# A two-layer vision tower with token routing: expert loads that wait for arithmetic instead of for written results, and a middle stage that begins three blocks later

## What is computed

```python
h = tok(x)                               # 64 patches of 28x28x3 through one matrix, class token, positions
h = h + attn0(layernorm(h))              # masked attention inside an image
h = h + ffn0(layernorm(h))               # 32 experts, 128 hidden, relu, the 2 best per token (sigmoid gates)
h = h + attn1(layernorm(h))              # |norm of (running sum - previous)| times a decaying sum of earlier tokens
h = h + ffn1(layernorm(h))               # 16 experts, 512 hidden, gelu, the 2 best per token (softmax gates)
```

## Time and profile before

| | us |
|---|---|
| three timed executions | 1088.7, 1091.51, 1091.65 (median 1091.51) |
| the profiled execution, its own time | 1087.39 |
| its span from first to last instruction | 1085.7 |
| busy in the span: PE / PEld / DVE / ACT / POOL | 914.5 / 772.5 / 847.8 / 503.9 / 678.9 |
| mean granted TensorE clock, as a share of 2.4 GHz | 0.909 |

### The profile page before, as it was taken

The page is one execution under the profiler, slowest core; times in us unless marked ns, Lnnn a source line. Parts: engine busy times, 40 slices in busy tenths (PEclk is TensorE's granted clock), DMA queues, the critical chain, the costliest instruction groups (busy, mean ns, idle before and its releaser), DMA issues.

```text
span 1085.7 us, 21714 instructions
## 1 busy us (share of the span) xinstructions
PE 914.5 (84%) x6064; PEld 772.5 (71%) x6064; DVE 847.8 (78%) x3318; ACT 503.9 (46%) x1342; POOL 678.9 (63%) x622
## 2 busy tenths in 40 slices
PE   6999999999999987476776877778569999999992
PEld 2577666677777666475665766677469989999992
DVE  1488889898888998666677899888667877778983
ACT  1355555555555442211112554777435655556561
POOL 1016666666676645677677767777777775545553
PEclk9999999999999997578887988877769999999996
DMA  9956566655566304577779973865188688889986
GB/s 371 353 206 217 202 217 222 222 201 201 201 206 211 123 21 116 152 209 206 210 219 310 293 259 120 265 228 169 59 302 263 231 253 277 275 279 301 356 325 235
DMA packets 118664, 246.57 MB, mean 227 GB/s; under 512 B 20914, under 2 KB 85936, under 8 KB 112400
## 3 DMA queue, kind: packets, MB, share of 16 engines
q1 hardware_dynamic: 77440, 191.26, 52.7%
q0 software_dynamic: 18592, 34.68, 9.4%
q10 hardware_dynamic: 22512, 19.25, 5.8%
HBM read 201.68 MB, written 45.43 MB: 228 GB/s over the span
## 4 chain that ended last, share of the span: by engine, by line
PE 39%; DVE 20%; issue 11%; DMA 11%; ACT 7%; SPq 6%; POOL 4%; ACTq 1%; DVEq 0%; POOLq 0%
PE ps L1032 6%; DMA xin<-lists_L 4%; PE ps L1010 4%; PE ps L762 4%; DMA results_L<-xin 3%; PE ps L1130 3%; POOL results_L L2582 3%; PE ps L829 3%; PE ps L1133 3%; PE ps L813 2%; SPq L614 2%; SPq L616 2%; PE ps L786 2%; SPq L607 2%; ACT x_hi L1211 2%
## 5 line engine op out<-in xcount | busy, mean ns | idle before, releaser
L2554 POOL DMA_INDIRECT lists_L<-rows,slots x230 | 263.4, 1145 | 153.3 <-issue 151.7
L2582 POOL DMA_INDIRECT results_L<-xin x145 | 146.2, 1008 | 96.3 <-DVE xin L2184 64.0
L2582 POOL DMA_INDIRECT results_L<-xin,place x146 | 144.1, 987 | 58.8 <-issue 39.3
L762 PE MATMUL ps<-xin,w_emb 128*128 128x512 f32 x292 | 137.7, 608 | 9.9 <-DMA w_emb<-in_w_main 8.3
L1032 PE MATMUL ps<-xin,QK 128*128 128x128 f32 x838 | 115.5, 289 | 2.6 <-DVE xin L2184 2.5
L1032 PEld LDWEIGHTS ps<-xin,QK 128*128 128x128 f32 x838 | 107.8, 204 | 4.5 <-issue 4.1
L2563 POOL TENSOR_TENSOR x_lo<-xin,x_hi 128x2048 fp32r<-128x2048 f32 x13 | 60.1, 4623 | 63.5 <-ACT x_hi L1219 63.1
L987 PE MATMUL ps<-ident,xin 128*128 128x128 f32 x291 | 66.3, 309 | 38.2 <-DMA xin<-lists_L 35.1
L1408 ACT ACTIVATE QK<-ps,xin 128x256 f32<-128x256 f32 x164 | 64.3, 475 | 70.9 <-PE ps L1010 70.9
L762 PEld LDWEIGHTS ps<-xin,w_emb 128*128 128x128 f32 x292 | 52.8, 194 | 58.9 <-issue 48.1
L2158 DVE TENSOR_SCALAR xin<-xin 128x128 f32<-128x128 f32 x291 | 92.7, 367 | 0.6
(11 more groups left out here) (408 smaller groups left out, 2436.4 us busy)
## 6 DMA issues: line engine op xcount, KB each, us to landing
xin<-in_x_main SPq DMA_DIRECT2D x48, 1536.0 KB, 6.7
xin<-in_w_L SPq DMA_DIRECT2D x81, 578.0 KB
xin<-in_w_L SPq DMA_DIRECT2D x98, 128.0 KB
xin<-lists_L SPq DMA_DIRECT2D x64, 132.0 KB
xin<-in_w_L ACTq DMA_DIRECT2D x65, 128.0 KB
x_hi<-results_L SPq DMA_DIRECT2D x13, 640.0 KB, 6.3
xin<-in_difference SPq DMA_DIRECT2D x13, 640.0 KB
xin<-in_distance SPq DMA_DIRECT2D x13, 640.0 KB, 6.6
```

What stands on the lines that cost most here:

```text
L762: mm = pe.matmul(psE[h], w_emb[:, k, :], xin[h][c][:, n, :], start=(k == 0), stop=False, skip_group_check=True)
L2554: pool.indirect_dma_start(out=lists[l.name], out_offset=bass.IndirectOffsetOnAxis(ap=slots_of(l, g, h)[:, t, k:k + 1], axis=0), in_=buf[:, ...
L2582: pool.indirect_dma_start(out=results[l.name], out_offset=bass.IndirectOffsetOnAxis(ap=where, axis=0), in_=yblk[u][:, q, :], in_offset=Non ...
```

## The change

Five edits, three of them in the way L1 blocks are fed:

1. `EARLY` is three blocks later: 48, 51, 57, 63, 69 instead of 45, 48, 54, 60, 66; `ALONE` goes with it.
2. DVE copies the places of L1 blocks too (81 more copies), and POOL's L1 results take their places from `place`.
3. The load of L1 block i waits for `y_ready` of block i-8, as that of L0 does, instead of `y_out`.
4. The fetches of finished results within the L1 blocks now wait for the landing of the results they read, which the waits of the loads before them had covered.
5. POOL does six instead of four scatters of group 11 before the first L1 result, and 14 instead of 16 between the results.

```diff
-        EARLY = {-3: 45, -2: 48, -1: 54, 0: 60, 1: 66}
+        EARLY = {-3: 48, -2: 51, -1: 57, 0: 63, 1: 69}
...
-            if l is L1:
-                eng.wait_ge(k.y_out[u], k.y0[u] + 16 * l.packets(i))
-            elif i >= l.unroll:
-                eng.wait_ge(k.y_ready, i - l.unroll + 1)
+            if i >= l.unroll:
+                eng.wait_ge(k.y_ready, k.i0 + i - l.unroll + 1)
...
-            sp_blocks(sp, L1, ends(load_end, 0))
-
-            def load_left(g, u, j):
+            def end_landed(g, u, j):
                 landed(L1, L1.enough(L1.class_of(g)))
                 load_end(g, u, j)
-            ends_left(load_left)
+            sp_blocks(sp, L1, ends(end_landed, 0))
+            ends_left(end_landed)
...
-                    if l is L0:
-                        dve.tensor_copy(place[:, u, :], xblk[u][:, :, PLACE].bitcast(U32))
+                    dve.tensor_copy(place[:, u, :], xblk[u][:, :, PLACE].bitcast(U32))
...
-                        where = place[:, u, q:q + 1] if l is L0 else xblk[u][:, q, PLACE:PLACE + 1].bitcast(U32)
-                            out=results[l.name], out_offset=bass.IndirectOffsetOnAxis(ap=where, axis=0),
+                            out=results[l.name], out_offset=bass.IndirectOffsetOnAxis(ap=place[:, u, q:q + 1], axis=0),
...
-                of = list(itertools.product((MG - 2, MG - 1), range(TILES * TOP)))[4:]
+                of = list(itertools.product((MG - 2, MG - 1), range(TILES * TOP)))[6:]
...
-            send(L1, MG - 2, MG % 2, 0, 4)
+            send(L1, MG - 2, MG % 2, 0, 6)
```

## The result

| | before | after |
|---|---|---|
| timed executions, median of five each | 1091.51 | 1083.02 |
| lowest and highest | 1088.14, 1091.93 | 1080.57, 1084.28 |
| profiled execution, its own time | 1087.39 | 1084.28 |
| its span | 1085.7 | 1082.5 |
| TensorE's mean granted clock | 0.909 | 0.903 |

The ratio is 0.9935, 95% interval 0.9915 to 0.9954: 0.65% or 7.1 us faster (the medians differ by 8.5, which lies within the interval). The forecast was 1084.5. The profiled executions differ by 3.1 us only: that of before lies 4.1 us under its median, that of after 1.3 above. So the two traces show where time moved, but not by themselves how large it is on average; the experiments give that.

The account below looks back on a forecast made before the run. Limits differ by stage: DVE, then POOL, then PE in L1, where late loads starve it and set the end. Terms -6.5 + 0 + 0 + 0 - 0.5 = -7.0 took 1091.51 to 1084.5 us; range 1080.0 to 1091.0.

Parts of the forecast that it names:

- Edits 2 and 3: L1 blocks: loads waiting for arithmetic, not landed results, remove PE's 11 waits for rows; -6.5 us, between 0 and -7.0.
- The copies: 81 place copies on DVE, 13.3 us of work, hidden before its waits for PE: 0, at most 1.6 us.
- up to 2.5 us later: L1 results on POOL: landing delay if the skill page's DVE lock held for these copies; loads would no longer wait for them.
- Edit 5: Start of L1 on POOL: two more scatters, 2.56 us, fit its 2.49 us idle before the first result: 0; uncovered 2.6.
- the one wait before load 24: L1: load 24's wait for scatters, left alone by the loads' edit; scatters would end up to 2.6 us sooner.
- Edit 4: SP in L1: waits for landings before fetches cost 0; at worst part of the 7.0 returns at few blocks.
- Edit 1: Middle stage three blocks later: start 5.2 us later, 4.7 given back, shorter stall -1.0; net -0.5, bounds -4.1 to +7.7.
- the shorter stall: DVE's 4.06 us idle before the first gather shortens because SP gets more head start: -1.0 us.
- B: Middle stage: the three blocks are only half given back, so the shift costs +2.9; net -3.6, 1087.9 us; chance 0.18.
- C: L1 loads: bound by transfers, so earlier loads only take longer; gain -1 to -3.5, near 1089 us; chance 0.12.
- D: Middle stage: group 1's slots come too late, POOL idles from about 668; net +1.2 to +4.4, 1092.7 to 1095.9; chance 0.08.
- E: L1: SP held by new landing waits or its fetches, loads start as late as before; 1091.51 within 1 or 2; chance 0.07.

Follow-up runs that it names:

- shift_only: The kernel before with only EARLY and ALONE three blocks later (48): 1091.53 us against 1089.46 for before timed together, ratio 1.0027.
- late_loads: The change with its L1 loads waiting for landed results again, all else as in the change: 1092.03 us, ratio to before 1.0029.

## Why the prediction was right, point by point

The time, 1084.5 forecast and 1083.02 measured, and the direction were right. Its terms were not as good as their sum.

**Edits 2 and 3, -6.5: the mechanism held, its size was off by 4.7.** Load 22 was to start at about 858.5, right behind the arithmetic; it starts 0.22 us behind it. PE's waits for rows were to fall under 1 us; none is left. But the gain is 11.1 to 11.2 us. The step that failed was "every one of the 11 waits should go, 7.0 us in all. At the most it is those 7.0": I took PE's row of waits as the upper end. It counts the times in which PE's records show a gap, 7.0 us in 11 times. PE's weight loads wait for the same DMAs in another row, which I had not used:

```profile
PEld ps L987 <- DMA xin<-lists_L: 10.8, 17, 2.1
```

That is 10.8 us in 17 times, of which 10.3 in 16 lie within the stretch, close to the 11.1 that came back. The two rows differ wait by wait. Before block 22 the weight load stands idle for 2.10 us and the matmul for 1.91:

```profile
878.39 0.20 PEld L987 LDWEIGHTS ps<-ident,xin 128*128 128x128 f32 x2 [2.10 <-DMA xin<-lists_L]
878.40 0.44 PE L987 MATMUL ps<-ident,xin 128*128 128x128 f32 x2 [1.91 <-DMA xin<-lists_L]
```

Each wait is 0.19 us shorter in PE's row, and those of 0.33 us and less are missing from it. That fits a modelled end of the matmul before which reaches into the wait. PEld's row holds in the other kernels too: the stretches of shift_only, late_loads and the one with four ahead are 13.1, 11.2 and 3.3 us above 246.9, and their PEld waits for rows are 12.3, 10.7 and 3.3. The same shows in the count of matmuls: in 850 to 893 us the kernel with late loads has PE idle for 4.6 us, but gets through 325 matmuls where the change has 378, and the 53 that are missing are 6.0 us at the change's 43 us for 378:

```profile
850.00:893.00 43.00, 38.44 (x325) 37.16 (x325) 31.76 (x98) 23.16 (x54) 33.09 (x31) 1.00 0.75 251
```

```profile
850.00:893.00 43.00, 43.00 (x378) 43.00 (x378) 34.97 (x112) 26.19 (x64) 33.40 (x32) 1.00 0.80 254
```

**The copies, 0: right.** With them PE is full for the whole stretch. POOL's results take 1001 ns each with the copies beside all of them, 1008 and 987 before; the median of the L1 results is 978 ns before and after. The lock of which the Trainium skill warns on its page "SBUF — State Buffer", section "SBUF: two separate sides", does not show at a copy of two columns of 4-byte words; no run here had a wide copy to show it at. The prediction's "up to 2.5 us later" took that page's example as it stands. The same section says that a DMA is "blocked until DVE-end + ~115 ns", and for a copy of 0.16 us that is at most about 0.3 us, an estimate from the page's figure and the copy's median.

**Edit 5, 0: not right.** The cover held: the first result stands 1.9 us behind the first bias with four ahead and with six (809.94 and 808.04 before, 815.46 and 813.56 after). But the pause in the tail costs 1.9 us, which no row of before could have told. The sooner end of the scatters, which was to help "the one wait before load 24", helped nothing that a trace shows: with four ahead and early loads PE did not wait for block 24 either. The 0.5 us which edits 2 and 3 were to leave there are 0 in after.

**Edit 4, 0: right.** SP waits 37.3 us before fetches, but the longest of these waits, 11.6 us, stands behind its last load (1036.55), and no load behind a fetch made PE wait. In the window 970 to 1000 PE is full. No run had edit 4 alone.

**Edit 1, -0.5: the account held, its small balance not.** The fetch was to be issued at 580.0 and the gather at 586.6; they came at 581.43 and 588.17 in after, and the gather at 586.1 to 588.4 in the four kernels with 48. The three blocks were given back: in the change's repeat the gather is 7.7 us later than with 45 (588.42 and 580.68), the slots of group 1 stand at 664.09 and 664.11; in the first profile of after they are 2.9 later than before, and the run with 51 agrees with the repeat. What hardly came is the shorter stall: DVE idles 4.31 us before the gather in after and 4.06 before, and on average 4.2 us in the profiles with 48, 4.6 in those with 45, so 0.4 instead of the 1.0 forecast. So the term is 0 to +3 rather than -0.5. The sentence that "before that DVE and SP decide, not POOL" missed the edge at which 45 stood: it is POOL's last L0 result that frees a fetch of rows, and with 45 that fetch is already up to 0.95 us late.

The rivals: **B** (shift costs +2.9) is near what shift_only was timed at, but its mechanism, blocks given back by half, is refuted by the run with 51 and by the repeat of the change. **C** (bound by transfers) is refuted: loads start right behind the arithmetic, and PE is full with a DMA share of 0.80 and 0.89. **D** (group 1 too late) did not happen: slots of group 1 at 666.76 were below the 668 named, POOL started its scatters at 672.7 as before. **E** (loads no earlier) is refuted by the 0.22 us.

With the measured terms the sum is -11.2 + about 2 (shift) + 0 (copies) + 1.9 (pause in the tail): -7.3, where the timed ratio says -7.1 and the repeat, at 0.9911, -9.7. The mechanism of edit 3 was understood; that the sum came out so near is luck: a gain that was 4.7 too small stood against two costs, together about 4, that were not seen.

## What to carry to other kernels

A wait for a landed DMA that only protects a buffer's last reader can be moved to the reader's arithmetic once the few words which the DMA still reads are copied elsewhere; here 81 small copies in idle time bought 11 us. Take the size of a stall not from one engine's row of waits: compare the weight loads' row, and the number of matmuls in a window with that of a window that is full. When a wait moves a stretch's length, look in the timeline at which block it stands before naming its cause: here it was at block 8, behind the paddings, and not at load 24. And before a table of starting points is moved, look for a short wait that has just appeared on the way of a dependent fetch: the move from 45 to 48 cost at most 3 us, the one from 45 to 42 cost 15.

## What was not expected of the hardware

POOL paused 1.6 us (five scatters ahead), 3.4 (six) or 3.6 (eight) without any releaser in the profile, 30 indirect DMAs after another such pause of 1.8 to 2.1 us, and its place followed the order of scatters and results exactly, through all repeats. One more pause, of 2.2 to 2.4 us before POOL's 52nd DMA from the end, stood at the same place in all thirteen profiles, whatever the order, so the order does not rule all of them. The one that moves was hidden wherever POOL had time to spare, and cost 1.9 us where it fell four DMAs before the end. 32 more instructions on POOL did not move it. The cause is open.

With the stage three blocks later TensorE's granted clock in the stretch 645 to 672 us was 0.67, 0.68, 0.68 and 0.76 in the four profiles with 48. It was 0.70 to 0.88 in the seven with 45, and 0.81 with 51. The engine was thus, on average, at 1.2 GHz for a larger part of that stretch with 48, but the two groups overlap. The lowest of the 45s, 0.70, is the kernel with eight scatters ahead. Its `t_entry` is 799.33 all the same, and that of shift_only, at 0.76, 798.89. So the clock there does not by itself make a late `t_entry`; what made that of after stays open.
